# Scores of 48 units computed keys by queries, turned by VectorE and a DRAM exchange

## The reference

```python
q = rope((layernorm(x) @ Wq)); k = rope(ctx @ Wk); v = ctx @ Wv      # 32, 8, 8 heads
scores = einsum('bhqd,bhkd->bhqk', q, k) / sqrt(D)                   # 128 x 128 per sequence and head
attn = softmax(where(mask == 0, -1e9, scores))                       # over keys
x = x + tanh(g_xattn) * (einsum('bhqk,bhkd->bhqd', attn, v) @ Wo)
x1, x2 = split(layernorm(x) @ w12.T + b12)
return x + tanh(g_ffn) * ((silu(x1) * x2) @ w3.T + b3)
```

## Time and profile before

| | |
|---|---|
| median of 3 runs | 644.98 us (642.45 to 645.43) |
| profiled execution | 644.58 us, its span 642.8 us |
| PE busy | 632.7 us, 98% |
| DVE busy | 512.7 us, 80% |
| POOL busy | 450.8 us, 70% |
| ACT busy | 316.5 us, 49% |
| DMA | 93.23 MB, q1 45.0% of 16 engines |

### The profile page before, as it was taken

One profiled execution on the slowest core, in us unless ns is written; L12 is line 12 of the kernel. 1 busy time (PEld: TensorE's weight loads), 2 busy tenths in 40 slices (PEclk: granted clock), 3 DMA queues, 4 the chain that ended last, 5 costly groups with the idle time before them and its releaser, 6 DMA issues.

```text
span 642.8 us, 10433 instructions
## 1 busy us (share of the span) xinstructions
PE 632.7 (98%) x3105; PEld 526.7 (82%) x3105; DVE 512.7 (80%) x1235; ACT 316.5 (49%) x891; POOL 450.8 (70%) x374
## 2 busy tenths in 40 slices
PE   8999999998999999999999999999999999999997
PEld 7888888786888888788888778888888888888886
DVE  3987665898988898889888888889887998985342
ACT  4435622545555555554555446555554557555210
POOL 6457866998888987898898788888887667502000
PEclk9999999999999999999999999999999999999999
DMA  9997995254454444436444354535434404100002
GB/s 301 318 332 212 305 301 163 90 173 139 164 156 133 152 144 147 132 132 192 138 144 147 119 162 149 164 116 174 137 114 134 131 0 114 37 2 0 1 33 98
DMA packets 101735, 93.23 MB, mean 145 GB/s; under 512 B 8240, under 2 KB 78384, under 8 KB 101680
## 3 DMA queue, kind: packets, MB, share of 16 engines
q1 hardware_dynamic: 100256, 91.52, 45.0%
q0 software_dynamic: 384, 1.05, 0.5%
q10 hardware_dynamic: 1040, 0.00, 0.1%
HBM read 60.30 MB, written 32.24 MB: 144 GB/s over the span
## 4 chain that ended last, share of the span: by engine, by line
PE 96%; DVE 1%; issue 1%; DMA 1%; ACT 0%; SPq 0%; DVEq 0%
PE f_bank L603 13%; PE f_bank L605 12%; PE f_bank L604 12%; PE o_bank L603 10%; PE o_bank L605 10%; PE o_bank L604 10%; PE s_banks L726 6%; PE pv_bank L603 3%; PE pv_bank L605 3%; PE pv_bank L604 3%; PE s_banks L727 2%; PE t_bank L603 1%; PE t_bank L605 1%; PE s_banks L605 1%; PE s_banks L604 1%; PE t_bank L604 1%
## 5 line engine op out<-in xcount | busy, mean ns | idle before, releaser
L1015 ACT ACTIVATE prob<-prob,small 128x128 f32<-128x128 f32 x256 | 99.7, 391 | 40.3 <-DVE small L1559 40.0
L603 PE MATMUL f_bank<-xT_hi,wq_hi 128*128 128x512 f32 x256 | 103.1, 403 | 0.3 <-DVE t_sin L1467 0.3
L603 PE MATMUL o_bank<-wo_hi,o_hi 128*128 128x512 f32 x248 | 98.4, 397 | 2.9 <-issue 2.4
L605 PE MATMUL f_bank<-xT_hi,wq_lo 128*128 128x512 f32 x256 | 100.1, 391 | 0.0
L604 PE MATMUL f_bank<-xT_lo,wq_hi 128*128 128x512 f32 x256 | 100.1, 391 | 0.0
L605 PE MATMUL o_bank<-wo_hi,o_lo 128*128 128x512 f32 x248 | 97.2, 392 | 0.0
L604 PE MATMUL o_bank<-wo_lo,o_hi 128*128 128x512 f32 x248 | 96.8, 390 | 0.0
L945 ACT ACTIVATE pT_hi<-p 128x512 fp32r<-128x512 f32 x51 | 32.3, 634 | 126.6 <-DMA p<-p_scratch 126.6
L1283 POOL TENSOR_TENSOR q<-t_cos,t_sin 128x512 f32<-128x512 f32 x64 | 82.9, 1295 | 16.5 <-DVE t_sin L1467 16.3
L1467 DVE TENSOR_TENSOR t_sin<-f_bank,rope 64x512 f32<-64x512 f32 x128 | 88.1, 688 | 2.7
L1292 POOL TENSOR_TENSOR prob<-prob,small 128x512 f32<-128x512 f32 x64 | 66.6, 1041 | 29.1 <-DVE small L1569 28.7
(11 more groups left out here) (173 smaller groups left out, 1472.1 us busy)
## 6 DMA issues: line engine op xcount, KB each, us to landing
p_scratch<-p_blk SPq DMA_DIRECT2D x51, 256.0 KB, 2.1
p<-p_scratch SPq DMA_DIRECT2D x51, 256.0 KB, 3.1
k_scratch<-ks_parts SPq DMA_DIRECT2D x16, 512.0 KB, 3.1
raw<-in_L_xattn_Wq_dram SPq DMA_DIRECT2D x32, 256.0 KB, 2.9
raw<-in_L_xattn_Wo_dram SPq DMA_DIRECT2D x32, 256.0 KB, 2.7
k_parts<-k_scratch SPq DMA_DIRECT2D x16, 512.0 KB, 4.8
v_scratch<-vs_hi SPq DMA_DIRECT2D x16, 256.0 KB, 3.9
v_scratch<-vs_lo SPq DMA_DIRECT2D x16, 256.0 KB, 4.1
```

Of the source, the lines that this page charges most:

```text
L603: nc.tensor.matmul(dst, st[0], mv_[0], start=start, stop=False)
L605: return nc.tensor.matmul(dst, st[1], mv_[0], start=False, stop=stop)
L1015: e = nc.scalar.activation(prob[:, k, h, :], prob[:, k, h, :], ACT.Exp, bias=nmin[k][:, h:h + 1], scale=-1.0, accum_out=psum_row[k][:, h:h ...
```

## The change

For units 4 to 51 (`turned`) the scores are computed keys x queries: the key part is the stationary operand, all four heads' queries (512 columns) the moving one, three matmuls into one bank. DVE transposes 32 x 32 blocks out of that bank (`score_blocks`) into `s_blk`; SP stores them to DRAM and loads them back with the blocks exchanged (`store_s`, `load_s`) into `s32`. The mask step is then one instruction per head that adds `s32` and a mask copy `mfill2` with its columns reordered, both in SBUF (`mask_turned`); `mask_first` falls away for these units. So that the turned scores come out in order, `add_q` (and `add_k`) writes q and k of these units with its columns interleaved (`apart`), and the transposes of the probabilities read contiguous columns. PE does `out_proj` of n-3 and `pv` of n-2 in a step, one unit later than before; the loops of all engines are `step(n)`.

```diff
+        def turned(n):
+            return ST0 <= n < ST1          # 4 <= n < 52
+        def apart(t):
+            return t.rearrange("p (b j a) -> p b a j", b=HB, j=4)
...
@@ SP
+            def store_s(n):
+                k, slot = n % 2, n % 4
+                sp.wait_ge(dve_sblk, n + 1 - ST0)
+                sp.dma_start(s_dram[slot * 128:(slot + 1) * 128, :], s_blk[:, k, :]).then_inc(s_stored[k], 16)
+            def load_s(n):
...
+                sp.dma_start(s32[:, k, :].rearrange("p (j x) -> p j x", j=4),
+                             s_dram[slot * 128:(slot + 1) * 128, :].rearrange("(j b) (i x) -> (b i) j x", j=4, i=4)).then_inc(s_loaded[k], 16)
@@ PE, scores
+                if turned(n):
...
+                        pe.wait_ge(dve_sblk, n - 1 - ST0)
+                    three(s_banks[:, 512 * k:512 * k + 512], (k_parts[:, half, b, 0:S], k_parts[:, half, b, S:2 * S]),
+                          (q_hi[:, k].rearrange("p h s -> p (h s)"), q_lo[:, k].rearrange("p h s -> p (h s)")), True, True).then_inc(pe_score, 1)
+                    return
@@ PE
+            def step(n):
+                scores(*u(n + 1))
+                q_block(0, n + 6)
+                out_proj(*u(n - 3))
+                pv(*u(n - 2))
@@ POOL, add_q
-                nc.gpsimd.tensor_tensor(q32[:, (e // 4) % 2, e % 4, :], t_cos[:, ts, :], t_sin[:, ts, :], ALU.add).then_inc(pool_rope, 1)
+                dst, c, s = q32[:, (e // 4) % 2, e % 4, :], t_cos[:, ts, :], t_sin[:, ts, :]
+                if turned(16 * gg + 4 * (e // 4)):
+                    dst, c, s = apart(dst), together(c), together(s)
+                nc.gpsimd.tensor_tensor(dst, c, s, ALU.add).then_inc(pool_rope, 1)
@@ DVE
+            def score_blocks(gg, c, k):
...
+                nc.vector.transpose(s_blk[:, k, :].rearrange("p (i h a) -> p i h a", i=4, h=GH),
+                                    s_banks[:, 512 * k:512 * k + 512].rearrange("p (h i b) -> p i h b", h=GH, i=4)).then_inc(dve_sblk, 1)
+            def mask_turned(gg, c, k):
...
+                scores = s32[:, k, :].rearrange("p (j h a) -> p h j a", j=4, h=GH)
+                fill = mfill2[:, n % B, :].rearrange("p (j a) -> p j a", j=4)
+                for h in range(GH):
+                    op = nc.vector.tensor_tensor_reduce(prob[:, k, h, :].rearrange("p (j a) -> p j a", j=4), scores[:, h], fill, 1.0, HUGE,
+                                                        ALU.add, ALU.min, nmin[k][:, h:h + 1])
...
+                keys = prob[:, k].rearrange("p h (j a) -> p j h a" if turned(n) else "p h (a j) -> p j h a", j=4)
```

More of the change, by code:

```diff
@@ L221, in unit, with u, together, masked_turn @@
             return (2 * c + k + d) // 2, (2 * c + k + d) % 2
+        def u(n):
+            return n // 16, n // 2 % 8, n % 2
         def on_pe(n):
-            return isinstance(n, int) and (n < HEAD_T or n >= 4 * UNITS - TAIL_T)
+            return n < HEAD_T or n >= 4 * UNITS - TAIL_T
+        def turned(n):
+            return ST0 <= n < ST1
+        def apart(t):
+            return t.rearrange("p (b j a) -> p b a j", b=HB, j=4)
+        def together(t):
+            return t.rearrange("p (b a j) -> p b a j", b=HB, j=4)
+        def masked_turn(n):
+            return n + 1 if n < ST0 else n + 1 - (ST1 - ST0)
         def turn_of(n):
@@ new lines, in step @@
+            def step(n):
+                G, r, k = n // 8, n // 2 % 4, n % 2
+                if turned(n + 1):
+                    store_s(n + 1)
+                if n >= 1 and not on_pe(n - 1):
+                    load_p(*u(n - 1))
+                if turned(n + 1):
+                    load_s(n + 1)
+                if n >= 1:
+                    load_next_chunk(n - 1)
+                if k == 1 and r == 0 and G > 0:
+                    next_v(1, G)
+                if k == 1 and r == 1:
@@ L538, in _ @@
             load_chunk(0, 2)
[L539 to L542, removed]
+            for n in range(0, 52):
+                step(n)
             def bias_load(h):
@@ L798, in _ @@
             scores(0, 2, 0)
[L799 to L804, removed]
+            for n in range(4, 52):
+                step(n)
             def h_tile(b):
@@ L856, in down @@
                 mm.then_inc(pe_down, 1)
-            q_block(3, 10)
+            pv(3, 1, 0)
+            out_proj(3, 0, 1)
+            q_block(0, 58)
             scores(3, 2, 1)
-            q_block(3, 11)
+            q_block(0, 59)
             pv(3, 1, 1)
@@ L1325, in _, with step @@
                         first_chunk(s)
[L1327 to L1333, removed]
+            def step(n):
+                add_q(0, n + 5)
+                split_chunk(*pair_chunks(*u(n - 1)[:2])[(n - 1) % 2])
+                q_lo_split(*u(n + 2))
+                norm(*u(n))
+                pT_lo_split(*u(n - 1))
             split_chunk(*pair_chunks(0, 0)[0])
@@ L1351, in _ @@
             pT_lo_split(0, 1, 0)
[L1352 to L1355, removed]
-                for c in range(2, 10):
-                    step(gg, c, 0)
-                    step(gg, c, 1)
+            for n in range(4, 52):
+                step(n)
             def ffn_lo(t):
@@ L1642, in _ @@
             add_out(0, 0, 0)
-            mask_scores(0, 2, 0)
+            score_blocks(0, 2, 0)
             cos_q(0, 9)
             sin_q(9)
-            recip(0, 2, 0)
-            p_blocks(0, 2, 0)
-            add_out(0, 0, 1)
-            for gg in range(3):
-                for c in range(2, 10):
-                    step(gg, c, 0)
-                    step(gg, c, 1)
+            for n in range(4, 52):
+                step(n)
             def ffn_tile(t):
```

182 lines of the change are left out of this document (112 added, 70 removed).

## The result

The changed kernel takes 737.11 us (median of 4 runs, 735.52 to 738.48) against 644.68 (642.45 to 645.43) of the kernel before on the same chip: 1.144 times as long, 95% interval 1.140 to 1.148. 721 was forecast, with a range of 648 to 757. The profiled run spans 736.7 us.

The account below looks back on a forecast made before the run. PE, holding 96% of the chain, bounded the kernel before; the change would make masks and POOL take turns at the port: 644.58 + 73.8 for 48 units at 8.7 us + 3 for the ends, 721 us, range 648 to 757.

Parts of the forecast that it names:

- The port, instruction by instruction: Mask step: DVE with two SBUF inputs and POOL take turns per instruction; 8.7 us a unit, 721 us, chance 0.60.
- One sign: POOL in the loop: chunk and q_lo 0.2 us longer than 1.29 in most units.
- The port kept over four masks: Rival, mask step: DVE keeps the port over all four masks; 666 us (0.13) or 640 us (0.07), chance 0.20.
- the port without effect for the custom instruction: Rival, mask step: the port does not matter for the custom mask instruction; PE bounds at 6.91, 635 us, chance 0.14.
- PE gives back 0.19 us a unit: Scores on PE: three matmuls of 0.68 us replace eight of 0.87 us; 48 x 0.19 = 9 us.
- Transposes 0.70: DVE: score transpose out of PSUM 0.70 us, upper end 1.11; probability transpose falls from 1.11 to 0.70.
- The strided write of the q sum at no price: POOL's q sum, inner stride of 32 elements: taken as 0 extra; upper end 0.75 us, step 9.3 us, 750 us.
- The exchange hidden in the slow case: Score exchange in the likeliest case: lands at 9.7, needed at 12.4, hidden with 2.7 us to spare.
- the fast case: Port of no matter, PE's pace 6.91 us: the exchange is tight, 9.7 against 10.6.
- the third rival: Exchange late: landing 2 us later costs about 1 us a unit, 685 us; chance 0.06 including anything dearer than 757.
- The ends, +3 (bounds 0 to 6): Loop ends: first mask waits once for the exchange, PE carries one out_proj and one pv into the tail; +3 us.
- loop term: The 48 changed units: 48 x 8.7 = 417.6 us less 343.84, +73.8 us.

Follow-up runs that it names:

- e3: The kernel before with one mask-instruction input moved from PSUM to SBUF, reading the mask in place of the hi*hi products; 765.36 us (single run).
- e1: The changed kernel with the mask columns copied by ACT into a free PSUM bank, so the masks have one SBUF input; 668.14 us.
- e10: e9 without ACT's copy of the mask columns to PSUM, so the masks read both inputs from SBUF again; 740.43 us.
- e5: The changed kernel with the four mask instructions of a unit replaced by one addition over 512 columns and one minimum; 698.51 us.
- e6: The changed kernel with POOL's low part of the weights' chunk cut to 32 of 512 columns from the second weight group on; 707.72 us.
- e7: e1 plus two moves at the loop's ends (664.03 us), with ACT's pT_hi and POOL's pT_lo moved into the next step; 661.35 us.
- e9: e8 with SP issuing the next weights' chunk load between the scores' store and the probabilities' load; 635.47 us.
- e8: e7 with the end of the loop written in another order, for units 49 to 53 alone; 650.21 us.

## Why the prediction was right

- **The port, instruction by instruction: right, and shown** by e3, e1, e10 (the same input moved in and out of SBUF in three kernels) and by e5 and e6 (one hand-over less, 0.6 and 0.9 us a step). The step fits in its parts: set to 0 at the reciprocal's end (338.97), the chunk starts at 3.59 (3.57 forecast), mask 2 is issued at 4.97 (4.9), mask 3 at 6.26 (6.06 + 0.21 = 6.27), the next reciprocal ends at 8.66 (8.67). One sign was off: the chunk and `q_lo` were to be 0.2 us longer than 1.29 and last 1.29 and 1.33. That the 48 units agree to 0.5 us is partly an offset: the usual step is 8.66 instead of 8.7, and a few longer ones (up to 10.94) make up the difference. The port kept over four masks and the port without effect for the custom instruction are both refuted by the 1.20 and 1.36 us rows.
- **PE gives back 0.19 us a unit:** too little, if anything. Steps that wait for nothing take 6.80 in e7 to e9, where 6.91 was worked out: the scores give back the 0.19 (0.68 against 0.87 us), and the matmuls around them the rest. The gain shows only once the masks no longer wait.
- **Transposes 0.70:** 717 and 712 ns; the upper end 1.11 was not needed.
- **The strided write of the q sum at no price:** 1307 against 1292 to 1303 ns of the plain ones. (The Trainium skill, "GPSIMD Engine Reference", section "Performance pitfalls for Q7 kernels", speaks of strided reads; this row shows that a write in steps of 32 elements does not pay it.)
- **The exchange hidden in the slow case:** right, the masks wait for it 2.3 us in all, once. In the fast case it is late, as the third rival had it for a pace near 6.9: in e7 the masks wait 17 us for it.
- **The ends, +3 (bounds 0 to 6): the term that was mis-sized.** They measured 19.7: 1.8 ahead of unit 4 and 17.9 behind unit 52. Added to a loop term of 74.3 (73.8 forecast) they are the whole distance from 721 to 737. The step said that PE carries an `out_proj` and a `pv` over and counted one wait, that of the first mask, which measured 2.3 and lies within the 48 units. It left out that the hand-written order of the tail was made for a `pv` one unit earlier. On DVE the reciprocal of unit 52 stood behind an `o_lo` whose `pv` was now late, and the next `o_lo`, for which PE waits 4.25 us, behind a weight tile that waits for its load:

```profile
581.67 0.69 DVE L1481 TENSOR_TENSOR o_lo<-pv_bank,o_hi 128x512 fp32r<-128x512 f32 x1 [4.05 <-ACT o_hi L994]
582.28 0.17 DVE L1656 RECIPROCAL small<-small 128x4 f32<-128x4 f32 x1
...
588.64 0.71 DVE L1745 STREAM_TRANSPOSE w_all<-raw 128x512 f32<-128x512 f32 x1 [3.94 <-DMA raw<-in_L_ffn_w_dram]
```

Of the 17.9 us, 9.3 are the four waits shown, 3.5 the work carried over, and 5.1 remain. The granted clock of the stretch (560.74 to 599.24) is 0.87, 1.00 in the kernel before. As an estimate, 38.5 us at that mean are 10 us at half rate, a loss of 5. e8 shows that the order was the cause of most of it: another order, nothing else, takes 12 us off this stretch of e7, and the granted clock is 1.00.

What stays open: why about a third of e10's steps run at half rate after a wait of 1.8 us, while others after the same wait (1.83 us ahead of 466.36) do not.

## What to carry to other kernels

When an operand of a VectorE instruction moves from PSUM to SBUF, look at what GpSimd runs at that moment: with two SBUF inputs each instruction can wait for a whole GpSimd one, so four short ones cost more than one long one, and a copy of the smaller operand into PSUM (0.26 us on ScalarE here) buys it back. When a pipeline gets a unit deeper, go through the hand-written order behind the loop as carefully as through the loop: here it cost 18 us, of which another order gave 12 back. And when a stall goes, expect the transfer beside it to be next; the order in which SyncE issues loads and stores was worth 11 to 15 us at the same bytes.

## What the runs showed of the hardware

- DVE with two SBUF inputs and POOL take turns after every single instruction, both ways, also for the custom one: the masks of 1.20 and 1.36 us wait for one POOL instruction each, and `q_lo` in e5 (1.73 us) for one DVE addition. POOL lets DVE in some 0.1 to 0.2 us ahead of its recorded end: the first mask ends at 344.00, so with 0.28 us of own work it would have started at 343.72, and the chunk ends at 343.85.
- TensorE at half rate after waits, in a kernel that ran at granted clock 1.000 before: the row of windows for 142.6 to 159.5 us of the changed kernel (PE, PEld, DVE, ACT, POOL busy, granted clock, DMA share, GB/s) has a clock of 0.70. PE stands still for 5.14 us there, is granted 0.50 behind that (154.00 to 156.00), and its twelve matmuls of `out_proj` take 4.55 us; behind a wait of 1.59 us they take 2.84 (346.44 to 349.28).

```profile
142.60:159.50 16.90, 11.39 (x33) 8.58 (x34) 11.51 (x20) 4.44 (x13) 10.43 (x9) 0.70 0.62 187
```
